# Decoder layer, cross attention in split float32: the six products of a step taken chunk by chunk instead of term by term

## The chip, the cores and the metric

The kernel runs on one core of one Trainium2 chip. The metric is the time of one execution on the device in microseconds (us). Lower is better.

## What is computed

One pre-norm decoder layer over `x` of 16 x 100 x 128, with a context of 16 x 1444 x 96. It has three sublayers with a residual each: causal self attention with rotary embedding (one head of 128), cross attention with 16 heads of 64 over the context, and a ternary feed-forward product. All of it is float32. The part that the change touches is the cross attention:

```python
q = (x @ Wq).reshape(B, Nq, h, dh)
k = (context @ Wk).reshape(B, Nk, h, dh)
v = (context @ Wv).reshape(B, Nk, h, dh)
scores = jnp.einsum('bqhd,bkhd->bhqk', q, k) * scale
attn = jax.nn.softmax(scores, axis=-1)
out = jnp.einsum('bhqk,bkhd->bqhd', attn, v).reshape(B, Nq, h * dh)
return out @ Wo + bo
```

## The kernel before

The weights are folded first: `M` is Wq times Wk of each head and `G` is Wv times Wo, so that scores are products of a 96-wide query with the context itself, and values are products of the softmax numerators with the context itself. To keep float32 accuracy with the faster `float32r` operand type, each operand is split into a high part and a low part (`q_hi`/`q_lo`, `cT_hi`/`cT_lo` for the context transposed, `cN_hi`/`cN_lo` for the context as it is, `pr_hi`/`pr_lo` for the softmax numerators), and each product is made of three terms: high with high, high with low, low with high. An extra row or column number 97 carries the negative row maximum into the scores and the sum of the numerators into the values; so some operands have 97 rows or columns and the others 96.

The main loop runs over 16 batches and 24 steps in each, 384 in all. A batch has 16 heads x 100 = 1600 queries in 4 blocks of 400 (`BLK`), and 12 chunks of 128 keys; a step takes one block and two chunks, `a` = 0 and 1, so a block has 6 steps. In a step `s` TensorE (PE) issues

- `scores` (line 1066): three pieces `i`, each with two products of 400 columns. Piece `i` is term `i` for chunk 0 and then for chunk 1. The stationary operand is a slice of `cT_hi` or `cT_lo`, the moving one the query block. Chunk 0 goes into one PSUM bank and chunk 1 into the next. The last product raises `st_ready`.
- `values` (line 1093) for the step two before (`LAG`): three pieces again, term by term, chunk 0 and then chunk 1. The stationary operand is a slice of `cN_hi` or `cN_lo` and the moving one the numerators. All go into one bank, `OUT`, over the six steps of a block. In the first step of each block chunk 0 is the short last chunk, stacked with its own low part, so that it takes a single product (done in piece 2) and the step has four value products instead of six.
- between the six pieces, `fill` (line 919): small products for the next batch (row maxima, queries, self attention) and the previous one (output projection). They go through three further banks, and VectorE empties these.

ScalarE waits for `st_ready` and takes the exponential twice, into `pr_hi` (line 629, then `hi_done`) and in place in the bank (line 631). VectorE subtracts them into `pr_lo` (line 888, then `lo_done`). On PE, `scores` of step `s` waits for `lo_done` of step `s` - 2, since the two score banks of that step are used again; `values` waits for `hi_done` of its step ahead of piece 0 and for `lo_done` ahead of piece 2. After the loop come the two last `values`, with no scores between them, and then the end of the last batch (`TAIL`).

The order of PE is the order of the program; no scheduler changes it. Every product is one call, and the trace shows a weight load (LDWEIGHTS, engine PEld) and a MATMUL for each.

Of the kernel before, what the change touches and what calls it, by code (L numbers as in the profile page):

```python
# [37 lines left out]
def decoder_layer(nc, x_in, ctx_in, ctx_last_in, ctxT_in, wself_in, wqT_in, wkT_in, wvT_in, wo_in, bo_in,  # L38
# [5 lines left out]
    NK, DC = ctx_in.shape[1:]  # L44
# [5 lines left out]
    FULL = NK // P  # L50
# [3 lines left out]
    BLK = 4 * S  # L54
    PAIR = 2 * BLK
    NB = Q // BLK
    BSTEPS = NCH // 2
    STEPS = NB * BSTEPS
    FILLS = 3
    LAG = 2  # L60
    RING = 3
    QT = -(-Q // P)
    FIRST = -(-PAIR // P)
# [15 lines left out]
    with ExitStack() as stack:  # L79
# [87 lines left out]
        ST, OUT, MISC, SIDE = 0, 4, 6, 5  # L167
# [750 lines left out]
        def _(pe):  # L918
# [147 lines left out]
            def scores(b, par, s, i):  # L1066


                blk = s // BSTEPS
                if s == 0 and i == 0:  # L1070

                    if isinstance(b, int) and b == 0:
                        pe.wait_ge(row_a_in_s, 16)
                    else:
                        pe.wait_ge(row_in_s, (b + 1) * 32)
                    pe.wait_ge(cTlo_done, b + 1)
                if blk == 2 and s % BSTEPS == 0 and i == 0 and isinstance(b, int) and b == 0:
                    pe.wait_ge(row_in_s, 32)
                if i == 0:
                    at_least(pe, lo_done, b * STEPS + s - 1)  # L1080
                for a in range(2):
                    c = chunk(s, a)
                    keys = slice(c * P, (c + 1) * P)
                    terms = [(cT_hi[par][0:DC + 1, keys], q_hi[par][0:DC + 1, :]),
                             (cT_hi[par][0:DC, keys], q_lo[par][:, :]),
                             (cT_lo[par][:, keys], q_hi[par][0:DC, :])]
                    k, q = terms[i]
                    mm = nc.tensor.matmul(banks[:, ST + 2 * (s % 2) + a, 0:BLK], k, q[:, blk * BLK:(blk + 1) * BLK],  # L1088
                                          start=(i == 0), stop=(i == 2))
                if i == 2:  # L1090
                    mm.then_inc(st_ready, 1)

            def values(b, par, s, i):

                blk, first = s // BSTEPS, s % BSTEPS == 0
                r = s % RING
                if s == 0 and i == 0:
                    pe.wait_ge(cNhi_done, b + 1)
                    pe.wait_ge(cNlo_done, b + 1)
                    pe.wait_ge(last_done, b + 1)  # L1100
                if i == 0:
                    if first:
                        at_least(pe, o_evac, b * NB + blk)
                    pe.wait_ge(hi_done, b * STEPS + s + 1)
                if i == 2:
                    pe.wait_ge(lo_done, b * STEPS + s + 1)
                for a in range(2):
                    c = chunk(s, a)
                    cols = slice(a * BLK, (a + 1) * BLK)
                    terms = [(cN_hi[par][:, c, 0:DC + 1], pr_hi, DC + 1), (cN_lo[par][:, c % FULL, :], pr_hi, DC),  # L1110
                             (cN_hi[par][:, c, 0:DC + 1], pr_lo, DC + 1)]
                    k, e, m = terms[i]
                    if c == FULL:

                        if i < 2:
                            continue
                        e = pr_hi
                    mm = nc.tensor.matmul(banks[0:m, OUT, 0:BLK], k, e[:, r, cols], start=(first and a == 1 and i == 0),  # L1118
                                          stop=(s % BSTEPS == BSTEPS - 1 and a == 1 and i == 2))
                if i == 2:  # L1120
                    mm.then_inc(pv_done, 1)

# [78 lines left out]
```

## Time and profile before

| | |
|---|---|
| median of 3 runs | 1144.6 us (1144.58 to 1145.0) |
| the profiled execution, own time | 1144.63 us |
| its span in the profile | 1142.8 us |
| VectorE (DVE) busy | 900.2 us (79%) |
| ScalarE (ACT) busy | 695.5 us (61%) |
| GpSimd (POOL) busy | 274.2 us (24%) |
| DMA | 43.22 MB, mean 38 GB/s |

The profile is of one execution. In it PE is the matmul engine and PEld the weight loads, which are issued by the same queue and overlap the products. A product's record is longer than its share of the engine, since products are pipelined; what one costs in a dense stream is the distance from its start to the start of the next. A stretch of the chain of waits that is all PE means that each product was followed by the next one and by nothing else.

### The profile page before, as it was taken

To read this page: it belongs to the slowest core of one execution; us is meant where nothing else is said; L and a number is where in the kernel's file an instruction comes from. 1 tells how busy PE (TensorE), PEld (TensorE's weight loads), DVE (VectorE), ACT (ScalarE), POOL (GpSimd) and SP (SyncE) were. 2 spreads that over 40 slices of the span, in tenths; PEclk is the share of its full clock that TensorE was granted. 3 is DMA by queue.
4 is the path that set the end of the run, shared out by engine and by line. 5 is a ranking of instruction groups with operands and counts; after the bars stand their busy time and mean duration, and the time that the engine had idled before them with its cause. 6 is when DMAs were issued, how large, how long until landed. Compare 5 with 4: busy or idle time off the path is not lost.

```text
span 1142.8 us, 17444 instructions
## 1 busy us (share of the span) xinstructions
PE 1113.0 (97%) x6377; PEld 1027.3 (90%) x6377; DVE 900.2 (79%) x1601; ACT 695.5 (61%) x1001; POOL 274.2 (24%) x350
## 2 busy tenths in 40 slices
PE   6699999999999999999999999999999999999996
PEld 5588999999999999999999999999999999999995
DVE  3698787887878798887878888787878878877544
ACT  1155756656565665756667566665757566575753
POOL 3220032321403232141222304122230322213020
PEclk9799999999999999999999999999999999999998
DMA  6101020111202011020201102020110202010000
GB/s 150 54 16 42 23 63 3 45 42 31 57 24 63 3 44 41 25 64 17 71 3 45 42 25 63 11 78 3 45 41 25 64 3 80 9 44 1 25 23 4
DMA packets 29027, 43.22 MB, mean 38 GB/s; under 512 B 9350, under 2 KB 24718, under 8 KB 28814
## 3 DMA queue, kind: packets, MB, share of 16 engines
q1 hardware_dynamic: 28942, 42.10, 13.6%
q8 instruction: 51, 0.84, 0.3%
q14 instruction: 34, 0.28, 0.1%
HBM read 30.97 MB, written 0.92 MB: 28 GB/s over the span
## 4 chain that ended last, share of the span: by engine, by line
PE 94%; DVE 4%; issue 1%; ACT 1%; DMA 0%; POOL 0%; POOLq 0%; DVEq 0%; ACTq 0%
PE banks L1088 37%; PE banks L1118 34%; PE banks L939 11%; PE banks L930 4%; PE banks L980 3%; PE banks L1023 1%; PE banks L959 1%; DVE maxes L680 1%; DVE maxes L688 1%; PE banks L1013 1%; PE banks L1051 0%; DVE pr_lo L888 0%; DVE xn L664 0%; PE banks L1000 0%; PE banks L992 0%
## 5 line engine op out<-in xcount | busy, mean ns | idle before, releaser
L629 ACT ACTIVATE pr_hi<-banks 128x800 fp32r<-128x800 f32 x384 | 322.4, 839 | 365.0 <-PE banks L1088 365.0
L680 DVE TENSOR_REDUCE maxes<-banks 128x1 f32<-128x482 f32 x585 | 371.7, 653 | 82.1 <-PE banks L939 77.2
L888 DVE TENSOR_TENSOR pr_lo<-banks,pr_hi 128x800 fp32r<-128x800 f32 x320 | 315.1, 985 | 58.9 <-ACT banks L631 57.2
L631 ACT ACTIVATE banks<-banks 128x800 f32<-128x800 f32 x384 | 319.8, 833 | 0.0
L939 PE MATMUL banks<-cT_hi,q_hi 96*128 96x482 f32 x585 | 223.5, 382 | 1.2 <-DVE maxes L680 1.2
L1088 PE MATMUL banks<-q_hi,cT_hi 97*128 97x400 f32 x768 | 215.9, 362 | 2.8 <-DMA q_hi<-negmaxT 2.5
L1118 PE MATMUL banks<-pr_hi,cN_hi 128*97 128x400 f32 x768 | 214.2, 346 | 0.1
L1088 PE MATMUL banks<-q_hi,cT_lo 96*128 96x400 f32 x768 | 208.3, 352 | 0.0
L1088 PE MATMUL banks<-q_lo,cT_hi 96*128 96x400 f32 x768 | 204.4, 347 | 0.0
L1118 PE MATMUL banks<-pr_lo,cN_hi 128*97 128x400 f32 x704 | 191.1, 345 | 0.0
L1118 PE MATMUL banks<-pr_hi,cN_lo 128*96 128x400 f32 x704 | 190.7, 345 | 0.0
L1088 PEld LDWEIGHTS banks<-q_hi,cT_hi 97*128 97x128 f32 x768 | 134.9, 191 | 13.3 <-issue 2.8
L1088 PEld LDWEIGHTS banks<-q_lo,cT_hi 96*128 96x128 f32 x768 | 143.5, 190 | 0.1
L1088 PEld LDWEIGHTS banks<-q_hi,cT_lo 96*128 96x128 f32 x768 | 138.4, 189 | 3.8
L479 POOL TENSOR_TENSOR ve<-mv,eps 100x1 f32<-100x1 f32 x48 | 9.2, 192 | 535.2 <-DVE mv L659 535.2
L1118 PEld LDWEIGHTS banks<-pr_hi,cN_hi 128*97 128x97 f32 x768 | 124.1, 163 | 12.5 <-issue 0.4
L1118 PEld LDWEIGHTS banks<-pr_hi,cN_lo 128*96 128x96 f32 x704 | 113.9, 162 | 17.2
L1118 PEld LDWEIGHTS banks<-pr_lo,cN_hi 128*97 128x97 f32 x704 | 114.3, 162 | 16.0
L939 PEld LDWEIGHTS banks<-cT_hi,q_hi 96*128 96x128 f32 x585 | 110.0, 188 | 8.8 <-DVE maxes L680 1.5
L496 POOL TENSOR_TENSOR cT_lo<-cT_raw,cT_hi 96x758 fp32r<-96x758 f32 x16 | 29.1, 1821 | 184.5 <-DMA rrow<-rsums 184.5
L512 POOL TENSOR_TENSOR o_st<-o_st,r_st 128x1200 f32<-128x1200 f32 x15 | 41.6, 2772 | 94.0 <-DMA r_st<-rrow 78.7
L930 PEld LDWEIGHTS banks<-x2T,M 128*96 128x96 f32 x512 | 56.6, 172 | 4.8 <-ACT G L599 1.0
(123 smaller groups left out, 889.0 us busy)
## 6 DMA issues: line engine op xcount, KB each, us to landing
cT_raw<-in_ctxT SPq DMA_DIRECT2D x16, 568.5 KB
cN_raw<-in_ctx SPq DMA_DIRECT2D x16, 528.0 KB
o_st<-o_sb SPq DMA_DIRECT2D x30, 150.0 KB, 2.3
r_st<-rrow SPq DMA_DIRECT2D x30, 150.0 KB, 2.7
o_st<-o_sb SPq DMA_DIRECT2D x30, 100.0 KB, 2.2
r_st<-rrow SPq DMA_DIRECT2D x30, 100.0 KB, 2.7
o_st<-o_sb SPq DMA_DIRECT2D x30, 50.0 KB, 2.0
r_st<-rrow SPq DMA_DIRECT2D x30, 50.0 KB, 2.6
```

What stands on the lines that cost most here:

```text
L496: nc.gpsimd.tensor_tensor(out=cT_lo[par][:, half:NT], in0=cT_raw[:, half:NT], in1=cT_hi[par][0:DC, half:NT].bitcast(F32), op=ALU.subtract) ...
L512: nc.gpsimd.tensor_tensor(out=o_st[:, :, :], in0=o_st[:, :, :], in1=r_st[:, :, :], op=ALU.mult).then_inc(on_done, 1)
L629: nc.scalar.activation(pr_hi[:, s % RING, :].rearrange("p (a q) -> p a q", a=2), pair, ACT.Exp, scale=float(DH) ** -0.5).then_inc(hi_done, 1)
L631: nc.scalar.activation(pair, pair, ACT.Exp, scale=float(DH) ** -0.5).then_inc(exp_done, 1)
L680: nc.vector.tensor_reduce(maxes[:, t, p:p + 1], here[:, 0:PW], AX.X, ALU.max).then_inc(misc_free, 1)
L688: nc.vector.tensor_reduce(maxes[:, t, p:p + 1], here[:, 0:PW], AX.X, ALU.max).then_inc(misc_free, 1)
L888: nc.vector.tensor_tensor(pr_lo[:, s % RING, :].rearrange("p (a q) -> p a q", a=2), banks[:, slot:slot + 2, 0:BLK], pr_hi[:, s % RING, :]. ...
L930: mm = nc.tensor.matmul(here[0:DC, i * S:(i + 1) * S], M[:, h, :], x2T[par][:, :], start=True, stop=True)
L939: mm = nc.tensor.matmul(here[:, 0:PW], q_hi[par][0:DC, qtile(t):qtile(t) + P], cT_hi[par][0:DC, PAT[p]:PAT[p] + PW], start=True, stop=True)
L980: mm = nc.tensor.matmul(here[0:S, 0:D], o_st[:, k, h * S:(h + 1) * S], G_st[:, k, h, :], start=(h == 0 and k == 0), stop=(h == 3 and k == ...
L1088: mm = nc.tensor.matmul(banks[:, ST + 2 * (s % 2) + a, 0:BLK], k, q[:, blk * BLK:(blk + 1) * BLK], start=(i == 0), stop=(i == 2))
L1118: mm = nc.tensor.matmul(banks[0:m, OUT, 0:BLK], k, e[:, r, cols], start=(first and a == 1 and i == 0), stop=(s % BSTEPS == BSTEPS - 1 and ...
```

## The change

The two loops of a step, over terms and over chunks, are exchanged. Three tables say which products (chunk, term) each of the three pieces holds: both terms that use the same chunk of the high context stand next to each other, and the low context follows. In `values` the terms are numbered anew (1 is now low numerators with high context, 2 high numerators with low context), the wait for `lo_done` moves from ahead of piece 2 to ahead of the second product of piece 0, and in the first step of a block the single product of the short chunk comes last.

```diff
+    ORDER = [[(0, 0), (0, 1)], [(0, 2), (1, 0)], [(1, 1), (1, 2)]]
+    ORDER_PV = [[(0, 0), (0, 1)], [(0, 2), (1, 2)], [(1, 0), (1, 1)]]
+    ORDER_FIRST = [[(1, 0), (1, 1)], [(1, 2)], [(0, 1)]]
...
-                for a in range(2):
+                for a, k in ORDER[i]:
...
-                    k, q = terms[i]
-                    mm = nc.tensor.matmul(banks[:, ST + 2 * (s % 2) + a, 0:BLK], k, q[:, blk * BLK:(blk + 1) * BLK],
-                                          start=(i == 0), stop=(i == 2))
+                    stationary, q = terms[k]
+                    mm = nc.tensor.matmul(banks[:, ST + 2 * (s % 2) + a, 0:BLK], stationary,
+                                          q[:, blk * BLK:(blk + 1) * BLK], start=(k == 0), stop=(k == 2))
...
-                if i == 2:
-                    pe.wait_ge(lo_done, b * STEPS + s + 1)
-                for a in range(2):
+                for a, k in (ORDER_FIRST if first else ORDER_PV)[i]:
+                    if i == 0 and k == 1:
+                        pe.wait_ge(lo_done, b * STEPS + s + 1)
...
-                    terms = [(cN_hi[par][:, c, 0:DC + 1], pr_hi, DC + 1), (cN_lo[par][:, c % FULL, :], pr_hi, DC),
-                             (cN_hi[par][:, c, 0:DC + 1], pr_lo, DC + 1)]
-                    k, e, m = terms[i]
-                    if c == FULL:
-
-                        if i < 2:
-                            continue
-                        e = pr_hi
-                    mm = nc.tensor.matmul(banks[0:m, OUT, 0:BLK], k, e[:, r, cols], start=(first and a == 1 and i == 0),
-                                          stop=(s % BSTEPS == BSTEPS - 1 and a == 1 and i == 2))
+                    terms = [(cN_hi[par][:, c, 0:DC + 1], pr_hi, DC + 1),
+                             (cN_hi[par][:, c, 0:DC + 1], pr_hi if c == FULL else pr_lo, DC + 1),
+                             (cN_lo[par][:, c % FULL, :], pr_hi, DC)]
+                    stationary, e, m = terms[k]
+                    mm = nc.tensor.matmul(banks[0:m, OUT, 0:BLK], stationary, e[:, r, cols],
+                                          start=(first and a == 1 and k == 0),
+                                          stop=(s % BSTEPS == BSTEPS - 1 and a == 1 and k == 1))
```

On PE, the last step but one of the last batch, before. Rows name the line, what is written from which operands, columns and the waits ahead of the product; x2 stands for two rows alike.

```order
L1088 MATMUL banks<-q_hi,cT_hi 128x400 [waits lo_done]
L1088 MATMUL banks<-q_hi,cT_hi 128x400
L1088 MATMUL banks<-q_lo,cT_hi 128x400 x2
L1088 MATMUL banks<-q_hi,cT_lo 128x400 x2
L1118 MATMUL banks<-pr_hi,cN_hi 97x400 [waits hi_done]
L1118 MATMUL banks<-pr_hi,cN_hi 97x400
L1118 MATMUL banks<-pr_hi,cN_lo 96x400 x2
L1118 MATMUL banks<-pr_lo,cN_hi 97x400 [waits lo_done]
L1118 MATMUL banks<-pr_lo,cN_hi 97x400
L992 MATMUL banks<-G,o_sb 100x128 [waits misc_free]
```

The same step in the changed kernel, where the lines stand three lower up to the scores:

```order
L1091 MATMUL banks<-q_hi,cT_hi 128x400 [waits lo_done]
L1091 MATMUL banks<-q_lo,cT_hi 128x400
L1091 MATMUL banks<-q_hi,cT_lo 128x400
L1091 MATMUL banks<-q_hi,cT_hi 128x400
L1091 MATMUL banks<-q_lo,cT_hi 128x400
L1091 MATMUL banks<-q_hi,cT_lo 128x400
L1117 MATMUL banks<-pr_hi,cN_hi 97x400 [waits hi_done]
L1117 MATMUL banks<-pr_lo,cN_hi 97x400 [waits lo_done]
L1117 MATMUL banks<-pr_hi,cN_lo 96x400 x2
L1117 MATMUL banks<-pr_hi,cN_hi 97x400
L1117 MATMUL banks<-pr_lo,cN_hi 97x400
```

The same twelve products stand there; three score products in a row now go to one bank, and the wait for the low part of the numerators stands ahead of the second value product instead of the fifth.

The last two `values` on PE, behind the last scores, before:

```order
L1118 MATMUL banks<-pr_hi,cN_hi 97x400 [waits hi_done]
L1118 MATMUL banks<-pr_hi,cN_hi 97x400
L1118 MATMUL banks<-pr_hi,cN_lo 96x400 x2
L1118 MATMUL banks<-pr_lo,cN_hi 97x400 [waits lo_done]
L1118 MATMUL banks<-pr_lo,cN_hi 97x400
L987 MATMUL banks<-cT_hi,o_sb 100x1 [waits o_evac,misc_free]
```

And in the changed kernel:

```order
L1117 MATMUL banks<-pr_hi,cN_hi 97x400 [waits hi_done]
L1117 MATMUL banks<-pr_lo,cN_hi 97x400 [waits lo_done]
L1117 MATMUL banks<-pr_hi,cN_lo 96x400 x2
L1117 MATMUL banks<-pr_hi,cN_hi 97x400
L1117 MATMUL banks<-pr_lo,cN_hi 97x400
L990 MATMUL banks<-cT_hi,o_sb 100x1 [waits o_evac,misc_free]
```

Shown is the last of the two; the one before it reads the same. Five products instead of two now stand behind the wait for `lo_done`.

## Rows read from the trace of the kernel before

**Rows 1.** The page: span, busy time, slices of PE and its clock, chain by line.
```profile
span 1142.8 us, 17444 instructions
PE 1113.0 (97%) x6377; PEld 1027.3 (90%) x6377; DVE 900.2 (79%) x1601; ACT 695.5 (61%) x1001; POOL 274.2 (24%) x350
...
PEclk9799999999999999999999999999999999999998
...
PE banks L1088 37%; PE banks L1118 34%; PE banks L939 11%; PE banks L930 4%; PE banks L980 3%; PE banks L1023 1%; PE banks L959 1%; DVE maxes L680 1%; DVE maxes L688 1%; PE banks L1013 1%; PE banks L1051 0%; DVE pr_lo L888 0%; DVE xn L664 0%; PE banks L1000 0%; PE banks L992 0%
```

**Rows 2.** Stretch 120 to 1100 us: length, then busy us (instructions) by engine, clock, DMA.
```profile
120.00:1100.00 980.00, 979.90 (x5713) 914.03 (x5712) 796.22 (x1402) 631.41 (x904) 242.87 (x290) 1.00 0.13 36
```

**Rows 3.** PE, groups of 120 to 1100 us: count, busy us, mean ns, idle us before.
```profile
L1118 PE MATMUL banks<-pr_hi,cN_hi 128*97 128x400 f32 x706 | 196.9, 346 | 0.1
L1088 PE MATMUL banks<-q_lo,cT_hi 96*128 96x400 f32 x706 | 187.1, 346 | 0.0
...
L1088 PEld LDWEIGHTS banks<-q_hi,cT_hi 97*128 97x128 f32 x706 | 124.0, 190 | 8.9
L1118 PEld LDWEIGHTS banks<-pr_hi,cN_hi 128*97 128x97 f32 x706 | 114.1, 163 | 11.1 <-issue 0.4 <-ACT o_sb L594 0.2
```

**Rows 4.** Timeline of PE, most of one step: start us, us of the row.
```profile
505.24 0.38 PE L939 MATMUL banks<-cT_hi,q_hi 96*128 96x482 f32 x1
505.46 0.53 PE L1088 MATMUL banks<-q_hi,cT_lo 96*128 96x400 f32 x2
505.82 0.38 PE L939 MATMUL banks<-cT_hi,q_hi 96*128 96x482 f32 x1
506.04 0.53 PE L1118 MATMUL banks<-pr_hi,cN_hi 128*97 128x400 f32 x2
506.40 0.53 PE L1118 MATMUL banks<-pr_hi,cN_lo 128*96 128x400 f32 x2
506.77 0.38 PE L939 MATMUL banks<-cT_hi,q_hi 96*128 96x482 f32 x1
```

**Rows 5.** Chain of waits in order of time: start us, us, what.
```profile
130.63 1.10 PE banks L1118 x6
132.42 1.12 PE banks L1088 x6
...
162.34 1.11 PE banks L1118 x6
...
172.04 1.10 PE banks L1088 x6
174.31 1.11 PE banks L1088 x6
...
176.83 1.14 PE banks L1088 x6
```

**Rows 6.** Line 1051, the start: seven tiles, three products each with one stationary tile.
```profile
L1051 PEld LDWEIGHTS banks<-cT_hi,q_hi x21: 186/329/337, 29.0 to 49.0; 96*128 96x128 f32 x21
```

**Rows 7.** Timeline of line 1051 on PE, two of a tile's three; the clock there.
```profile
38.53 0.60 PE L1051 MATMUL banks<-cT_hi,q_hi 96*128 96x482 f32 x2
...
38.50:39.10 0.60, 0.60 (x3) 0.20 (x2) 0.60 (x2) 0.60 (x3) 0.00 (x0) 1.00 0.00 0
```

**Rows 8.** Timeline of PE at half clock, the first step of the loop.
```profile
56.33 0.87 PE L1088 MATMUL banks<-q_lo,cT_hi 96*128 96x400 f32 x2
57.00 0.60 PE L943 MATMUL banks<-cT_hi,q_hi 96*128 96x482 f32 x1
...
55.50:57.50 2.00, 1.97 (x6) 1.91 (x7) 0.00 (x0) 0.00 (x0) 0.00 (x0) 0.50 0.69 199
```

**Rows 9.** Waits of PE for the low part: us in total, times, longest.
```profile
PE banks L1088 <- DVE pr_lo L888: 0.3, 1, 0.3
```

**Rows 10.** Timeline of PE and VectorE, the last two values of the kernel.
```profile
1128.36 0.98 DVE L888 TENSOR_TENSOR pr_lo<-banks,pr_hi 128x800 fp32r<-128x800 f32 x1
...
1128.93 0.55 PE L1118 MATMUL banks<-pr_hi,cN_hi 128*97 128x400 f32 x2
...
1129.64 0.99 DVE L888 TENSOR_TENSOR pr_lo<-banks,pr_hi 128x800 fp32r<-128x800 f32 x1 [0.30 <-ACT banks L631]
1129.68 0.53 PE L1118 MATMUL banks<-pr_lo,cN_hi 128*97 128x400 f32 x2
...
1130.05 0.52 PE L1118 MATMUL banks<-pr_hi,cN_hi 128*97 128x400 f32 x2
...
1130.68 0.26 PEld L1118 LDWEIGHTS banks<-pr_lo,cN_hi 128*97 128x97 f32 x2
1130.77 0.53 PE L1118 MATMUL banks<-pr_lo,cN_hi 128*97 128x400 f32 x2
```

## The prediction

> **What bounds the kernel now.** I read the head of the page first, then the stretches, the groups by line, the timeline of a step, and the chain of waits. The page [rows 1] shows PE busy for 97% of the span, and in its chain lines 1088 (scores) and 1118 (values) hold 37% and 34%; the reader is to see that these two lines are the ones the change reorders. The stretch from 120 to 1100 us [rows 2] shows PE busy for 979.90 of 980.00 us at a granted clock of 1.00, the 2.4 GHz level. So in the loop nothing is waited for: the time is the number of products times their spacing, and only a change of the spacing, or a wait that did not exist, can move it.
>
> The spacing is read from starts, not from the records, which last 346 ns for scores and values alike because they overlap [rows 3]. In one step [rows 4] two score products start at 505.46 and the next product at 505.82: 0.18 us each. Two value products from 506.04 to 506.40: 0.18. The products of 482 columns: 0.22 (505.24 to 505.46). The chain of waits gives it more finely [rows 5]: six score products take 1.10 to 1.12 us and six value products 1.10 or 1.11, thus 0.183 to 0.187 us for one. Four points in these rows matter for the change:
>
> - Scores alternate between two banks, values all go to one bank, and both have the same spacing.
> - Scores load 128 columns of weights (190 ns a load) and values 97 (163 ns) [rows 3], and the spacing is the same; so in these runs the load is not what sets it.
> - Products of neighbouring terms that share nothing (high with low context) are as close as the others.
> - Products that already share the whole stationary operand exist: at the start each query tile is multiplied with three pieces of the context, one after the other. There are 21 such products with 7 tiles, and the trace has 21 loads [rows 6], three for each tile. Two of them that follow each other at full clock take 0.60 us together [rows 7]; less the record of one such product, 0.38 [rows 4], that is 0.22 from start to start, the same as for the 482-column products in the loop, which have another stationary operand on either side.
>
> **The change part by part.**
>
> *The order of products.* Nothing is removed or added: an ordinary step keeps its twelve products, the first step of a block its ten, and every call still brings its own load by rows 6. What is new is who stands next to whom: in a step both chunks now have a pair with a common operand in the scores (97 rows in the first, 96 of the same in the second) and in the values (identical). That is 2 x 384 = 768 pairs in the scores and 2 x 384 - 64 = 704 in the values (64 first steps of a block have one instead of two), 1472 in all. By rows 7 a pair of this kind is worth 0.22 - 0.22 = 0, so I cost it at 0.
>
> The trace of before has no such pair in the loop, so I bound it. The most that a pair could give is the part of the spacing that isn't the columns themselves. At the 1.2 GHz level (granted 0.50) two score products start at 56.33 and the next at 57.00, 0.335 us each [rows 8]; at twice the clock this would be 0.167, and 0.183 is seen. So the bound is 0.016 us a pair. Below nothing I see no price in a shared operand as such.
>
> In the Trainium skill, the page "TensorE: Matmul & The Clock Gate", section "Step-by-step: what each phase is for", says that loading is separate so that one can load once and multiply repeatedly, and section "Back-to-back issue gap" gives columns / 2.4 GHz + 2.5 ns for a warm product in isolation. For 400 columns that is 169 ns, so by that page the sum would be 14 ns less for each pair whose second load falls away; rows 7 show neither a missing load nor a shorter spacing.
>
> *The banks.* In a step four of six score products now follow one into the same bank, where before none did. The value products always did so, and their six take 1.10 or 1.11 us against 1.10 to 1.12 [rows 5]. So I take 0. As bounds I take one unit of the last printed figure either way, 0.01 us on the six score products of a step: 384 x 0.01 = 3.8 us less or more.
>
> *The wait for the low part, in the loop.* It moves ahead by three products and whatever fills stand between. In a step `s` the scores, which come first on the same queue, already wait for the low part of step `s` - 2, and that is just the one which the values of the same step need. So at any place behind the scores the wait is already met, and its place costs nothing in 382 of the 384 values. The earlier wait itself cost PE 0.3 us once in the whole execution [rows 9]. No DMA, SP, POOL, ScalarE or VectorE instruction moves; `st_ready` and `pv_done` still hang on the last product of their six, so ScalarE and VectorE get their inputs at the same distance as before. The fills keep their slots, but for the first step of a block, where one fill comes one product (0.18 us) later; VectorE is busy for 796 of 980 us [rows 2] and PE does not stand still for it, so this is 0.
>
> *The wait at the end.* The last two values have no scores ahead of them. Before [rows 10], the low part of step 22 was ready at 1128.36 + 0.98 = 1129.34, and it was wanted at 1129.68: no wait. That of step 23 was ready at 1129.64 + 0.99 = 1130.63, the load that waited for it started at 1130.68, its product at 1130.77, thus 0.14 behind the end of VectorE, and the last product at 1130.77 + 0.18 = 1130.95. Now the second product of step 22 would be due at 1128.93 + 0.18 = 1129.11 and has to wait until 1129.34 + 0.14 = 1129.48; with five products from there step 23 begins at 1129.48 + 5 x 0.183 = 1130.40 instead of 1130.05. Its second product, due at 1130.58, again has to wait for the low part, until 1130.77. Behind it come four products instead of one: the last starts at 1130.77 + 4 x 0.183 = 1131.50. That is 0.55 us later than 1130.95, and everything to the end (evacuation, sums, output projection, feed-forward, store) hangs on it.
>
> **The sum**, against the profiled execution: 1144.63 us (span 1142.8) + 0 (pairs) + 0 (banks) + 0 (loop waits) + 0.55 (end) = **1145.2 us**. The profiled execution lies 0.03 us over the median of the runs shown, which changes nothing.
>
> **The rivals.** A measurement of this kernel can tell about 0.2% from no change, 2.3 us, so the limits are 1142.3 and 1146.9.
>
> *The change does what it says: the second load of a pair falls away or costs nothing, and products close up (faster).* Only the 704 identical pairs: 704 x 0.016 = 11.3 us, 1145.2 - 11.3 = 1133.9. With the scores too, 1472 x 0.016 = 23.6 us, 1121.6. By the page's 14 ns instead it would be 704 x 14 ns = 9.9 us, thus 1135.3. For it: PEld is busy for 914 of 980 us [rows 2], hardly less than PE. In the skill, "Trainium Kernel Development and Optimization", section "Best Practices", names LDWEIGHTS busy time, not that of products, as the measure of how near a kernel is to its limit, and by that rule dropping loads should pay here. Against it: rows 6 and 7, where loads of the same tile are all there and the spacing is what it is elsewhere, and the equal spacing with loads of 97 and 128 columns. I give it 0.04.
>
> *Three score products in a row into one bank (slower).* If a product that adds to the bank of the one just before has to wait for it, each of 4 x 384 = 1536 new neighbours in the score banks pays. The dearest six in the rows took 1.14 us against 1.11 [rows 5]; at 0.03 us a step that is 384 x 0.03 = 11.5 us and 1145.2 + 11.5 = 1156.7. It decides from (1146.9 - 1145.2) / 1536 = 1.1 ns a neighbour on. Against it: the values do just this, in all of their steps, at 1.10 or 1.11. I give it 0.04.
>
> *The pace of the score products shifts a little.* Most of the score sixes in the chain take 1.11 or 1.12, the value sixes 1.10 or 1.11. If scores in one bank took over the pace of values, up to 0.01 us a step, the time would be 1145.2 - 3.8 = 1141.4; the other way 1149.0. Between these ends I take the pace as it is, since the row nearest to it is the kernel's own score six. I give 0.09 to a shift down that passes 1142.3 and 0.05 to one up past 1146.9.
>
> **How the numbers follow.** The forecast, within 0.2%, has what is left: 1 - 0.04 - 0.04 - 0.09 - 0.05 = 0.78. Faster is 0.04 + 0.09 = 0.13, slower 0.04 + 0.05 = 0.09. The range takes in the forecast and both shifts of the pace, 1141.4 to 1149.0; the two outer rivals, 0.08 together, are left out.
>
> **What would show it.** In the profile after: 6377 loads and 6377 products again; PE busy for nearly all of 980 us from 120 to 1100; sixes of line 1091 and line 1117 in the chain at 1.10 to 1.12 us; the last value product at about 1131.5 us and the rest of the end 0.55 us later. Fewer loads, or sixes under 1.08 us, would show the first rival; score sixes of 1.13 us and over with value sixes unchanged the second; a line in the waits from line 1117 to the low part with more than 1 us would show that the wait isn't met in the loop after all.

## The result and the profile after

The changed kernel takes 1146.59 us (median of 20 runs, 1146.15 to 1147.48), the kernel before, beside it, 1144.57 (20 runs, 1144.16 to 1145.41). The ratio is 1.0017 with an interval of 1.0010 to 1.0024: 2.0 us more, against the 0.6 us of the prediction. It is just inside the 0.2% that the prediction counted as no change, and inside its range. The profiled execution took 1146.15 us with a span of 1144.4; the one before 1144.63 and 1142.8.

The head of the page after, to be held against [rows 1]:

```profile
span 1144.4 us, 17444 instructions
...
PE 1114.5 (97%) x6377; PEld 1027.6 (90%) x6377; DVE 900.0 (79%) x1601; ACT 695.5 (61%) x1001; POOL 273.5 (24%) x350
...
PEclk9799999999999999999999999999999999999998
...
PE banks L1091 37%; PE banks L1117 34%; PE banks L942 11%; PE banks L933 4%; PE banks L983 3%; PE banks L1026 1%; PE banks L962 1%; DVE maxes L683 1%; DVE maxes L691 1%; PE banks L1016 1%; DVE pr_lo L891 0%; PE banks L1054 0%; DVE maxes L833 0%; DVE xn L667 0%; PE banks L1003 0%
```

There are 6377 products and 6377 loads, as before: no load fell away. The clock is the same in every slice. The stretch of the loop, as [rows 2]:

```profile
120.00:1100.00 980.00, 979.93 (x5702) 913.84 (x5701) 795.04 (x1400) 631.08 (x904) 242.25 (x290) 1.00 0.13 36
```

PE is again busy from end to end at the 2.4 GHz level. In the same 980 us it now gets through 5702 products instead of 5713, eleven fewer. (What that is in time is measured below; the count also depends on whether short or long products stand at the edges of the stretch.) So the loop lost pace; it did not gain a wait. The waits of PE on the low part of the numerators say the same:

```profile
PE banks L1091 <- DVE pr_lo L891: 0.3, 1, 0.3
```

It is the row of [rows 9] again, at the scores, and no row of PE at line 1117 that waits for the low part stands beside it; the weight loads of line 1117 waited for it twice in all, and both waits are in the tail below:

```profile
PEld banks L1117 <- DVE pr_lo L891: 0.8, 2, 0.5
```

Each chunk's pair in the scores has a load for either product. The weight loads of line 1091, count, least/median/longest ns:

```profile
L1091 PEld LDWEIGHTS banks<-q_hi,cT_hi x768: 186/188/338, 55.1 to 1128.1; 97*128 97x128 f32 x192
...
L1091 PEld LDWEIGHTS banks<-q_lo,cT_hi x768: 188/190/337, 55.3 to 1128.3; 96*128 96x128 f32 x192
```

The chain of waits of the kernel after, from 172 to 178 us, as [rows 5]:

```profile
174.03 1.10 PE banks L1091 x6
175.35 1.09 PE banks L1117 x6
176.53 1.14 PE banks L1091 x6
177.88 1.09 PE banks L1117 x6
```

Piece by piece they hardly differ from those of [rows 5]. Only counted over the whole chain does a shift appear: of the 235 score sixes without a fill in them 1 took 1.13 us before and 22 do after, while those of 1.12 were 24 and are 4.

To split the 2.0 us I take two distances between starts on PE: the *loop*, from the first score product to the first score product of the last step, and the *end*, from there to the last value product. The loop's bounds, before:

```profile
55.53 0.67 PE L1088 MATMUL banks<-q_hi,cT_hi 97*128 97x400 f32 x1 [2.54 <-DMA q_hi<-negmaxT]
...
1126.65 0.43 PE L1088 MATMUL banks<-q_hi,cT_hi 97*128 97x400 f32 x1
```

And after:

```profile
55.12 0.67 PE L1091 MATMUL banks<-q_hi,cT_hi 97*128 97x400 f32 x1 [2.54 <-DMA q_hi<-negmaxT]
...
1127.65 0.43 PE L1091 MATMUL banks<-q_hi,cT_hi 97*128 97x400 f32 x1
```

With the traces' nanoseconds the loop took 1071.12 us before and 1072.52 after, **1.40 us more**, and the end 4.31 and 4.84, **0.53 us more**. Together that is 1.93 of the 2.0 us. (The start of the loop lay between 55.1 and 55.7 us in the executions profiled here, whatever the kernel; after's came 0.41 us earlier than before's, which is why its span grew by 1.5 us only.) Summed over the 6190 products of the loop as distances to the next product, the 1.40 us are +0.96 at the scores, -0.61 at the values, +0.73 at the fills of 482 columns, +0.25 at the fills of line 943 before, and 0.07 elsewhere.

The tail after, as [rows 10] (the last two values; idle time before a row in brackets):

```profile
1129.36 0.98 DVE L891 TENSOR_TENSOR pr_lo<-banks,pr_hi 128x800 fp32r<-128x800 f32 x1
...
1129.92 0.35 PE L1117 MATMUL banks<-pr_hi,cN_hi 128*97 128x400 f32 x1
1130.39 0.16 PEld L1117 LDWEIGHTS banks<-pr_lo,cN_hi 128*97 128x97 f32 x1 [0.49 <-DVE pr_lo L891]
...
1130.66 0.53 PE L1117 MATMUL banks<-pr_hi,cN_lo 128*96 128x400 f32 x2
...
1131.39 0.34 PE L1117 MATMUL banks<-pr_hi,cN_hi 128*97 128x400 f32 x1
1131.68 0.16 PEld L1117 LDWEIGHTS banks<-pr_lo,cN_hi 128*97 128x97 f32 x1 [0.31 <-DVE pr_lo L891]
...
1131.94 0.53 PE L1117 MATMUL banks<-pr_hi,cN_lo 128*96 128x400 f32 x2
...
1132.49 0.34 PE L1117 MATMUL banks<-pr_lo,cN_hi 128*97 128x400 f32 x1
```

Everything there stands 0.99 us later than before by the loop, which began 0.41 us earlier and took 1.40 us longer (the first value product of step 22 starts at 1129.92 instead of 1128.93). Less that, the first value product of step 23 is at 1130.40 and the last at 1131.50, both as predicted.

So the end was right and the pace of the loop was not: it was costed at nothing and took 1.4 us. The experiments ask where that came from. The theories at the outset: the order of the products itself (scores, values, or both), products into one bank, the shared operand, the moved wait, or no more than the program's place in memory.

### The profile page after: what moved, and what is told of

It is laid out like the page before. It is cut to its first block, busy times and chain, and to the rows that moved or that the text cites. A ratio compares the mean times of both kernels' runs of the same rounds, so it can differ in the third digit from the quotient of the medians.

```text
span 1144.4 us, 17444 instructions
## 1 busy us (share of the span) xinstructions
PE 1114.5 (97%) x6377; PEld 1027.6 (90%) x6377; DVE 900.0 (79%) x1601; ACT 695.5 (61%) x1001; POOL 273.5 (24%) x350
## 4 chain that ended last, share of the span: by engine, by line
PE 94%; DVE 4%; issue 1%; ACT 1%; DMA 0%; POOL 0%; POOLq 0%; DVEq 0%; ACTq 0%
PE banks L1091 37%; PE banks L1117 34%; PE banks L942 11%; PE banks L933 4%; PE banks L983 3%; PE banks L1026 1%; PE banks L962 1%; DVE maxes L683 1%; DVE maxes L691 1%; PE banks L1016 1%; DVE pr_lo L891 0%; PE banks L1054 0%; DVE maxes L833 0%; DVE xn L667 0%; PE banks L1003 0%
## 5 line engine op out<-in xcount | busy, mean ns | idle before, releaser
L1091 PE MATMUL banks<-q_hi,cT_hi 97*128 97x400 f32 x768 | 279.2, 364 | 2.8 <-DMA q_hi<-negmaxT 2.5
L1091 PE MATMUL banks<-q_lo,cT_hi 96*128 96x400 f32 x768 | 272.1, 354 | 0.0
L1117 PE MATMUL banks<-pr_hi,cN_hi 128*97 128x400 f32 x768 | 266.0, 346 | 0.1
L1091 PE MATMUL banks<-q_hi,cT_lo 96*128 96x400 f32 x768 | 264.6, 345 | 0.0
L1117 PE MATMUL banks<-pr_lo,cN_hi 128*97 128x400 f32 x704 | 242.8, 345 | 0.1
L1091 PEld LDWEIGHTS banks<-q_lo,cT_hi 96*128 96x128 f32 x768 | 146.6, 191 | 7.4
L1091 PEld LDWEIGHTS banks<-q_hi,cT_hi 97*128 97x128 f32 x768 | 145.5, 189 | 7.3 <-issue 2.8
L1091 PEld LDWEIGHTS banks<-q_hi,cT_lo 96*128 96x128 f32 x768 | 146.2, 190 | 2.8
```

The source lines that it names most:

```text
L1117: mm = nc.tensor.matmul(banks[0:m, OUT, 0:BLK], stationary, e[:, r, cols], start=(first and a == 1 and k == 0), stop=(s % BSTEPS == BSTEPS ...
```

## The experiments

Each line gives loop and end of the profiled execution, then the median with the ratio to the kernel before in the same batch (its median was 1144.56 to 1144.60 in all). The medians tell about 1 us, and they hold the start of the loop too, which moves by up to 0.55 us. Two pairs of kernels have the same program up to the end of the loop (after and e4, e3 and e8), and their loops differ by 0.05 us at most. But a loop figure is that of one execution, and an isolated wait in it counts in full, as e6 and e9 show; so where it matters loops are compared batch by batch or step by step, from the start of one step's first score product to that of the next, in the traces' nanoseconds.

| kernel | loop us | end us | median us | ratio |
|---|---|---|---|---|
| before | 1071.12 | 4.31 | 1144.57 | |
| after | 1072.52 | 4.84 | 1146.59 | 1.0017 [1.0010, 1.0024] |
| e1, the wait alone | 1071.46 | 4.86 | 1145.78 | 1.0010 [1.0001, 1.0019] |
| e2, the scores alone | 1072.05 | 4.29 | 1145.65 | 1.0009 [1.0001, 1.0018] |
| e3, the values alone | 1070.16 | 4.84 | 1144.19 | 0.9997 [0.9988, 1.0005] |
| e4, after with the old end | 1072.57 | 4.30 | 1146.03 | 1.0013 [1.0004, 1.0022] |
| e5, one stationary operand for six | 1069.93 | 4.31 | 1143.42 | 0.9990 [0.9981, 0.9999] |
| e6, scores by chunk without pairs | 1072.84 | 4.29 | 1145.76 | 1.0010 [1.0002, 1.0019] |
| e7, tiles 32 bytes further | 1070.87 | 4.29 | 1144.37 | 0.9998 [0.9989, 1.0007] |
| e8, values alone with the old end | 1070.11 | 4.29 | 1143.62 | 0.9991 [0.9982, 1.0000] |
| e9, scores by chunk, banks in turn | 1072.40 | 4.29 | 1145.61 | 1.0011 [1.0002, 1.0020] |
| e10, scores by term, three to a bank | 1071.11 | 4.31 | 1144.39 | 1.0000 [0.9991, 1.0009] |
| e11, values by chunk without pairs | 1069.56 | 4.30 | 1143.01 | 0.9986 [0.9977, 0.9994] |
| e12, after with 97 rows everywhere | 1069.58 | 4.85 | 1143.65 | 0.9992 [0.9983, 1.0001] |

### e1: the wait alone

Order as before; only the wait for the low part goes ahead.

```diff
-                if i == 2:
-                    pe.wait_ge(lo_done, b * STEPS + s + 1)
                 for a in range(2):
+                    if i == 0 and a == 1:
+                        pe.wait_ge(lo_done, b * STEPS + s + 1)
```

> The order of products is that of before; only the wait for the low part moves ahead of the second value product. Measured so far: loop (start of the first score product to that of the last step) 1071.1 us before, 1072.5 in the changed kernel; end (that last start to the last value product) 4.31 and 4.84 us. Theory A (the wait costs only in the last two values, the rest of the +2.0 us comes from the order): loop 1071.1, end 4.84, time +0.55 us. Rival B (the wait is met in the loop, but a load with a wait is prepared later and so costs some ns in each step): loop 1072.5, end 4.84, time +2.0 us.

The end grew from 4.31 to 4.86 us, the loop by 0.34 us. So the end's 0.55 us hang on the wait's place and on nothing else, and the wait is met in the loop: a wait that held PE up in its 382 earlier values would not be had for 0.34 us. Compared step by step, 346 of the 383 steps agree with before's within 2 ns. The 0.34 us lie in few of the others: 0.11 at one step of the last batch, 0.08 at one of batch 4, and most of the rest in pieces of some twenty nanoseconds. So the wait does not slow the steps of the loop; why those few are longer was not found. (The median rose by 1.2 us, 0.3 more than loop and end together; the profiled execution is the fastest of its eleven, with a loop that began 0.27 us earlier than before's.)

### e2 and e3: the scores alone, the values alone

e2 takes the order table of the scores and their part of the change, e3 the two tables of the values, their part and the moved wait.

```diff
+    ORDER = [[(0, 0), (0, 1)], [(0, 2), (1, 0)], [(1, 1), (1, 2)]]
...
-                for a in range(2):
+                for a, k in ORDER[i]:
...
```

> Only the score products go chunk by chunk, values and their wait as before. Theory A with the pace lost in the scores: loop 1072.5 us or a little more, end 4.31, time +1.4 us. Rival B (the wait in the loop): loop 1071.1, end 4.31, time +0. Rival C (the pace is lost in the values): loop 1071.1, time +0.

```diff
+    ORDER_PV = [[(0, 0), (0, 1)], [(0, 2), (1, 2)], [(1, 0), (1, 1)]]
+    ORDER_FIRST = [[(1, 0), (1, 1)], [(1, 2)], [(0, 1)]]
...
-                if i == 2:
-                    pe.wait_ge(lo_done, b * STEPS + s + 1)
-                for a in range(2):
+                for a, k in (ORDER_FIRST if first else ORDER_PV)[i]:
+                    if i == 0 and k == 1:
+                        pe.wait_ge(lo_done, b * STEPS + s + 1)
...
```

> Only the values and their wait are changed, the scores are those of before. Theory A: loop 1071.1 us or up to 0.5 us less, end 4.84, time +0.1 to +0.55 us. Rivals B and C: loop 1072.5, end 4.84, time +2.0 us.

The loop of e2 is 0.93 us longer than before's, that of e3 0.96 us shorter. So the scores' new order costs, and the values' new order gives a little; no theory had expected either size. The two do not add up: -0.03 together, and +1.40 measured. The parts act on each other, in the spacing of the fills between them above all (those of 482 columns, on the mean of batches 1 to 14, counted from 0: 219.3 ns to the next product before, 219.8 in e2, 218.8 in e3, 220.8 after). A part of this is explained under e6 to e10; that the two orders cost more together than apart was not.

### e4 and e8: the old end

The last two values alone go by term again, with the wait where it was; e4 does this to the changed kernel, e8 to e3.

```diff
+    ORDER_END = [[(0, 0), (1, 0)], [(0, 2), (1, 2)], [(0, 1), (1, 1)]]
...
-                    if i == 0 and k == 1:
+                    if (a == 0 and k == 1) if end else (i == 0 and k == 1):
...
-                    values(B - 1, 1, s, i)
+                    values(B - 1, 1, s, i, True)
```

> The changed kernel, but the last two values go in the order of before with the wait where it was. Theory A: loop 1072.5 us as in the changed kernel, end back at 4.31, time +1.4 us against before. A rival for the end (the 0.5 us there come from the scores of the last step, not from the wait): end stays at 4.84, time +2.0 us.

> Values in the new order in the loop, the last two values and their wait in the old, scores as before. If the parts add up: loop 1070.16 us as in the run with the values alone, end 4.31, time 1144.6 - 1.0 = 1143.6 us. If not: 1144.2 or more.

The end goes back to 4.30 and 4.29 us and the loops stay (1072.57 and 1070.11 beside 1072.52 and 1070.16). The medians fall by 0.56 and 0.57 us, from 1146.59 to 1146.03 and from 1144.19 to 1143.62. The term of the end is shown from both sides.

### e5: one stationary operand for all six score products

The computation is cut: all six score products of a step take the high context of chunk 0 and the high part of the query, so the scores lack their low parts and chunk 1.

```diff
-                    k, q = terms[i]
+                    k, q = cT_hi[par][0:DC + 1, chunk(s, 0) * P:chunk(s, 0) * P + P], q_hi[par][0:DC + 1, :]
```

> Order of before, but all six score products of a step use one and the same stationary slice (high context, chunk 0) and one and the same moving block (high query): of the scores, the chunk 1 and the low parts are left out. The only run where sharing is taken to the end: five of six score products follow one with the same weights, 1920 pairs. Theory A (a shared operand is worth nothing, each product brings its load): 6377 loads, loop 1071.1 us give or take 4. Rival (a load of the same weights falls away or becomes cheaper, up to 0.016 us a pair): 1920 x 0.016 = 31 us less.

Six with the very same operands, stationary and moving, make 5 x 384 = 1920 pairs; in 1769 of them the two products follow each other directly on PE, in the others a fill stands between. The page of e5:

```profile
PE 1111.4 (97%) x6377; PEld 1025.4 (90%) x6377; DVE 900.0 (79%) x1601; ACT 695.6 (61%) x1001; POOL 274.3 (24%) x350
```

All 6377 loads are there. At the bound of 0.016 us a pair the loop would have lost 31 us, or 28 with the direct pairs alone; it lost 1.19. And for this 1.19 us e12 gives another reason below: all six have 97 rows here. Sharing the stationary operand is worth nothing in this kernel.

### e6, e9 and e10: pair, bank and order taken apart

e6 takes the scores by chunk, but between the two products that would share the high context it puts the one with the low context.

```diff
+    ORDER = [[(0, 0), (0, 2)], [(0, 1), (1, 0)], [(1, 2), (1, 1)]]
...
+                                          q[:, blk * BLK:(blk + 1) * BLK], start=(k == 0), stop=(k == 1))
```

> As the run with the scores alone by chunk (loop 1072.05 us), but within a chunk the low context stands between the two products of the high one: three in a row go to one bank, no neighbours share the operand. Theory A1 (the +0.9 us of the scores come from three products in one bank): loop 1072.0. Rival A2 (they come from the shared neighbours): loop 1071.1 or less. Rival A3 (neither: which moving and stationary blocks follow each other, by their places in memory): any loop from 1070 to 1073.

e9 has e2's order of operands, but sends the two products of a piece to the two banks in turn; terms of both chunks are mixed in a bank, so the scores are others than the reference's.

```diff
-                for a in range(2):
+                for at, (a, k) in enumerate(ORDER[i]):
...
+                    mm = nc.tensor.matmul(banks[:, ST + 2 * (s % 2) + at, 0:BLK], stationary,
+                                          q[:, blk * BLK:(blk + 1) * BLK], start=(i == 0), stop=(i == 2))
```

> Score products in the order of the changed kernel (chunk by chunk), values as before, but the six go to the two score banks in turn, as before; so each bank holds a mixture of terms of both chunks, which the reference does not have. Theory A1 (three products in a row to one bank cost the pace): loop back to 1071.1 us or less. Rival A3 (it is the sequence of operands): loop 1072.05 as in the run with the scores alone by chunk.

e10 is the opposite: the order of operands of the kernel before, the first three products to one bank, the last three to the other (again mixed).

```diff
-                    mm = nc.tensor.matmul(banks[:, ST + 2 * (s % 2) + a, 0:BLK], k, q[:, blk * BLK:(blk + 1) * BLK],
-                                          start=(i == 0), stop=(i == 2))
+                    mm = nc.tensor.matmul(banks[:, ST + 2 * (s % 2) + (2 * i + a) // 3, 0:BLK], k, q[:, blk * BLK:(blk + 1) * BLK],
+                                          start=((2 * i + a) % 3 == 0), stop=((2 * i + a) % 3 == 2))
```

> Score products in the order of before (term by term), but the first three of the six go to the first score bank and the last three to the second; again the terms are mixed. Theory A1: loop 1072.0 us or more. Rival A3: loop 1071.1.

e6 alone looked like the work of the banks: without pairs the loop still took 1072.84 us. e9 and e10 took that back. By term the loop is 1071.12 us with the banks in turn and 1071.11 with three in a row; by chunk it is 1072.40 and 1072.05.

The 0.79 and 0.35 us by which e6 and e9 exceed e2 are not the pace of the loop. They lie almost whole (0.77 and 0.33 us) at the end of batch 12 and the start of batch 13, at 934 to 942 us. There the first score product of batch 13 waited for the row of negative maxima, which a DMA brings; in e2 it did not wait. Why the DMA came later is not shown. The wait of PE in e6, from 934 to 938 us:

```profile
PE banks L1089 <- DMA q_hi<-negmaxT: 0.5, 1, 0.5
```

The loads of the same line, in e6 and then in e9:

```profile
PEld banks L1089 <- DMA q_hi<-negmaxT: 0.9, 1, 0.9
PEld banks L1089 <- DMA q_hi<-negmaxT: 0.4, 1, 0.4
```

Away from it the three loops are the same: over batches 2 to 11, 672 us, e6 and e9 differ from e2 by 1 ns at most. So do e10 and before over batches 2 to 14. e6 differs from e2 by the pairs, e9 from e2 and e10 from before by the banks. So a shared stationary operand and three products in a row to one bank both cost nothing and gain nothing; what costs the microsecond is something in the order that e2, e6 and e9 have in common.

Where in the six does it lie? Means over batches 1 to 14 of the distance from the start of each score product to the start of the next, ns:

| | 1 | 2 | 3 | 4 | 5 | 6 | sum |
|---|---|---|---|---|---|---|---|
| rows, by term | 97 | 97 | 96 | 96 | 96 | 96 | |
| before | 215.1 | 182.6 | 186.5 | 181.7 | 199.3 | 182.0 | 1147.2 |
| e10 | as before | | | | | | 1147.2 |
| rows, by chunk | 97 | 96 | 96 | 97 | 96 | 96 | |
| e2 | 215.2 | 185.6 | 181.7 | 185.7 | 200.1 | 181.8 | 1150.0 |
| e6 | 215.5 | 185.6 | 181.7 | 185.7 | 200.1 | 181.8 | 1150.3 |
| e9 | 215.5 | 185.6 | 181.7 | 185.7 | 200.1 | 181.8 | 1150.4 |
| after | 215.6 | 184.6 | 181.8 | 185.6 | 200.3 | 182.0 | 1150.0 |
| e5, all 97 rows | 215.3 | 182.2 | 182.2 | 182.2 | 198.8 | 181.6 | 1142.4 |
| e12, all 97 rows | 215.2 | 182.0 | 182.5 | 182.7 | 198.6 | 181.7 | 1142.7 |

(Positions 1 and 5 are long also because short fills ahead of them are caught up with there.) The distances of 186 stand exactly behind products that have another number of rows than the product ahead of them: position 3 by term, 2 and 4 by chunk. The others are 182, 96 after 96 as well as 97 after 97. In after position 2 loses part of it. Position 5 by chunk shows it in part: in the 199 steps of these batches without a fill ahead of it, 184.8 ns in e2 against 183.2 before. A first value product directly behind a score product, 128 rows after 96, shows about half: 184.2 ns before and 184.1 after, against 182.4 and 181.8 for a value product between two others. And the fills of 482 columns, which have 96 rows, show it: between two score products the next one follows after 217.5 ns before, where the product ahead of the fill has 96 rows, and after 222.2 ns in after, where it has 97. With 72 such fills in these batches that is 0.34 us of the 0.73 found at the fills. That made the next theory: not the bank, not the operand, but the change of the number of rows.

### e7: another place in memory

```diff
+        sb("shift", [P, 8])
```

An unused tile of 32 bytes ahead of the query tiles.

> The kernel before, with an unused tile of 32 bytes per partition ahead of the query tiles, so that every tile declared behind lies 32 bytes higher; program and order are the same. Theory A3 (the small differences in pace come from the places of the operands in memory): loop moves by 0.5 us or more, either way. Rival (the pace comes from the order and the banks): loop 1071.1 to 1071.5 as in the runs so far with this order.

The loop is 0.25 us shorter, outside both expectations. It is no scatter: in every second batch from 2 to 12 step 4 is 21 ns longer than before's, step 5 about 44 shorter and step 9 about 24 shorter. So the place in memory shifts the pace by a few tenths in the loop, but not by the 1.4 us in question, as far as one shift can tell. (It is not what e1's 0.34 us are; there no tile has another place.)

### e11: the values without pairs

On e8, the product with the low context is put between the two that share the high one.

```diff
-    ORDER_PV = [[(0, 0), (0, 1)], [(0, 2), (1, 2)], [(1, 0), (1, 1)]]
+    ORDER_PV = [[(0, 0), (0, 2)], [(0, 1), (1, 0)], [(1, 2), (1, 1)]]
...
-    ORDER_FIRST = [[(1, 0), (1, 1)], [(1, 2)], [(0, 1)]]
+    ORDER_FIRST = [[(1, 0), (1, 2)], [(1, 1)], [(0, 1)]]
...
-                    if (a == 0 and k == 1) if end else (i == 0 and k == 1):
+                    if (a == 0 and k == 1) if end else k == 1 and (a == 0 or first) and i < 2:
```

> Scores as before, values chunk by chunk, but within a chunk high with high, low context, low numerators, so that no neighbours share the stationary operand; the last two values as before. The run with pairs has loop 1070.1. Theory A (sharing is worth nothing; the small gain of the values comes from the sequence otherwise): loop 1070.1 give or take 0.3. Rival (the pairs make the gain): loop 1071.1 or more.

The little that the values gained (e8: 1.0 us) is not from sharing: without any pair it is more, 1.56 us, also more than the 0.3 us of play that theory A allowed. This kernel is the fastest of all, 1143.01 us, and one of two (with e5, whose scores are not those of the layer) whose interval against the kernel before lies wholly below 1. The order by chunk as such seems to suit the values; all of them have 128 rows, so a change of rows among them can't be the reason, and which of the remaining differences is (who follows whom, 96 or 97 columns of weights, what the fills come behind) stays open.

### e12: the changed kernel with 97 rows in every score product

The low parts of query and context get a 97th row of zeros, written once ahead of the loop, so that all score products have 97 rows. The sums stay the same.

```diff
-        q_lo = two("q_lo", [DC, Q], F32R)
+        q_lo = two("q_lo", [DC + 1, Q], F32R)
...
-        cT_lo = two("cT_lo", [DC, NCH * P], F32R)
+        cT_lo = two("cT_lo", [DC + 1, NCH * P], F32R)
...
+            for i in (0, 1):
+                constant(q_lo[i][DC:DC + 1, :], 0.0)
+                constant(cT_lo[i][DC:DC + 1, 0:NT], 0.0)
...
-                             (cT_hi[par][0:DC, keys], q_lo[par][:, :]),
-                             (cT_lo[par][:, keys], q_hi[par][0:DC, :])]
+                             (cT_hi[par][0:DC + 1, keys], q_lo[par][:, :]),
+                             (cT_lo[par][:, keys], q_hi[par][0:DC + 1, :])]
```

> The changed kernel, with a row of zeros added to the low query and the low context, so that all score products have 97 rows and none 96; the sums are the same, and four memsets of the rows run in idle time of GpSimd at the start. In all runs so far, by position in a step, the starts of the records show about 186 ns instead of 182 behind each score product that has another number of rows than the product before it (third of six when the order is by term; second and fourth, and in part fifth, when it is by chunk), whatever the banks and shared operands. Theory R (a change of the number of rows costs about 4 ns): the six scores take 7.6 ns less a step, as in the run with one weight; fills of 96 rows between them lose 2.4 ns; 384 x 5.2 ns = 2.0 us less, loop 1070.5 us against 1072.5, time +0 against before instead of +2.0. Rival (something else in the sequence, such as which blocks follow each other): loop 1072.5, time +2.0 us.

The theory of the rows held. The loop falls from 1072.52 to 1069.58 us, 2.94 less, where 1070.5 was expected; its bounds:

```profile
55.65 0.67 PE L1094 MATMUL banks<-q_hi,cT_hi 97*128 97x400 f32 x1 [2.54 <-DMA q_hi<-negmaxT]
...
1125.23 0.43 PE L1094 MATMUL banks<-q_hi,cT_hi 97*128 97x400 f32 x1
```

Of these, 3.11 us are at the scores, and the rest of the loop gives 0.17 back. The fills of 482 columns, for which a loss of 2.4 ns each had been expected, did not get slower on the mean of batches 1 to 14 (220.80 and 220.81 ns): the order by chunk had taken this from them already, since e5, by term with 97 rows everywhere, has 220.7 against before's 219.3. The distances of 186 ns are gone from the table above, and the chain of waits shows the sixes of e12, as those of after at the same place:

```profile
174.23 1.10 PE banks L1094 x6
175.56 1.09 PE banks L1120 x6
176.74 1.12 PE banks L1094 x6
178.07 1.09 PE banks L1120 x6
```

Counted over the whole chain, 177 of e12's 235 score sixes without a fill in them take 1.10 us or less and one takes 1.13; in after it is 102 and 22 of 235. In e12 the stretch from 120 to 1100 us holds 5724 products where after has 5702:

```profile
120.00:1100.00 980.00, 979.91 (x5724) 915.30 (x5723) 796.39 (x1404) 631.85 (x904) 242.53 (x290) 1.00 0.13 36
```

With the end still at 4.85 us, the median is 1143.65 us: 2.9 us under after. Against the kernel before its interval just touches no change. What was not tried is e12's row together with e11's values and the old end.

## Why the prediction was right, and the term that it mis-sized

*What bounds the kernel.* Right. PE is busy for 979.93 of 980 us after as before, and every microsecond of the difference in the loop is spacing.

*The pairs, 0.* Right. Loads stayed at 6377, also in e5 with six alike; at the bound e5 should have lost 31 us and lost 1.2, and the scores by chunk take the same time with and without pairs (e2 and e6, to 1 ns over ten batches). The count of 768 pairs in the scores was too high, since in 149 of the 384 steps a fill stands inside the second chunk's pair; at a price of 0 that changes nothing. The first rival fell. So did the estimate from the Trainium skill's page "TensorE: Matmul & The Clock Gate" (section "Back-to-back issue gap"): no product after a shared load started 14 ns sooner. And the Trainium skill's page "Trainium Kernel Development and Optimization", section "Best Practices", names the busy share of the loads, beside MFU (the share of peak arithmetic), as the measure of the distance to the limit. That the loads set the pace here, as the first rival took from it, the trace does not bear out: loads of 97 columns (163 ns) and of 128 (190 ns) [rows 3] go with the same spacing.

*The banks, 0.* Right: 1071.12 and 1071.11 us in one order, 1072.05 and 1072.40 in the other, and of these 0.35 us all but 0.02 are the late DMA of e9. The second rival fell. But the sign that the prediction gave for it appeared, score sixes of 1.13 us (22 of 235, 1 before) with no value six longer than before: the sign could not tell the banks from the order of the rows, and only e9 and e10 did.

*The waits in the loop, 0.* Right for the steps in general: e1 has 346 of 383 unchanged, and the 0.34 us of its loop stand in few of the others.

*The end, +0.55.* Right: +0.53 after, +0.55 in e1, gone in e4 and e8.

*The order of products, 0.* This term was mis-sized: it measured +1.4 us. The prediction asked of a new neighbour whether it shares the operand and whether it writes the same bank. It did not ask whether it has the same number of rows, though its own sentence had the numbers in it (97 rows in the first product of a pair, 96 in the second). By term the six have one change of rows within them, by chunk three, and behind such a product the next one starts about 4 ns later. At the scores themselves that made 2.8 ns a step, 0.96 us of the 1.40 in the loop, and at the fills behind them another 0.34. The rest, a gain at the values and further losses at the fills, stays unexplained, and with it why the scores alone cost 0.93 us, the values alone gave 0.96, and both together cost 1.40. The rival "the pace of the score products shifts a little" is what happened, upwards, by 1.4 of the 3.8 us that it allowed; so the range held. It gave this direction the smaller chance, and its reason was the banks, which do nothing. That the time stayed within 0.2% of no change, by 0.3 us, is in part luck: the scores' loss and the values' gain, each near 1 us, were not foreseen, nor that they would not cancel. As a bound the last printed figure of [rows 5], a hundredth of a microsecond on a six, was well chosen: the 2.8 ns are under that digit.

## What to carry to other kernels

Where PE runs from end to end and each product brings its own load, putting equal stationary operands next to each other buys nothing; look first whether loads fall away at all. Moving a wait ahead costs nothing while work ahead of it has waited for the same thing, so look for the places without that work, the last steps of the program. And keep the operand shapes of neighbouring products alike: a row of zeros that makes them equal took 2.9 us off the changed kernel, more than any order of operands gave here (1.6 us, e11). Part of the 2.9 us is what the order by chunk had cost; with equal rows in the order by term e5 gained 1.2 us in the loop.

## What was not expected of the hardware

- In these runs a product whose number of rows differs from that of the product ahead of it is followed a little later than one of equal rows, for 400 columns at the 2.4 GHz level: about 4 ns with 96 and 97 rows (186 against 182), about 2 ns with 128 after 96 (184 against 182). With equal rows the 4 ns are gone (e12). Why a change of rows costs time, the runs don't show.
- Neither a shared stationary operand nor the bank changes the pace by more than 1 ns in 672 us (e6 and e9 against e2). Six products with identical operands are no closer than six with different ones and equal rows (182.2 ns in e5, 182.0 to 182.7 in e12).
- Most steps repeat to 2 ns where two kernels have the same loop (353 of 383 in after and e4), so that parts of a microsecond in 1071 can be told from the trace, where medians of 11 runs tell about one. What does not repeat are isolated waits: one DMA that came late made 0.8 us in e6, and only the comparison step by step showed it.
